# All nine tap products kept in SBUF, planes 6 and 7 added by GpSimd ahead of the fold's reader, other places in the schedule

## The chip, the cores and the metric

The kernel runs on one core of a Trainium2 chip. The metric is the device time in microseconds of one execution, the median of several runs. The core has TensorE (matmuls, results in PSUM), VectorE, ScalarE, GpSimd, and SyncE (SP), which only issues DMAs here. Sixteen DMA engines serve all queues. Each engine works through its own instruction queue in order; semaphores tie the queues together.

## What is computed

The input x has the shape 32 x 64 x 56 x 56 in float32. Two layers are applied, each to a group-normalised copy of its input and added to it:

```python
def _L0_conv_ref(x, ...):                 # binary depthwise + pointwise
    h = sign(x)
    h = depthwise_conv3x3(h, sign(dw_weight))
    h = sign(bn1(prelu(h, prelu1_a)))
    h = einsum('bchw,oc->bohw', h, sign(pw_weight))
    h = bn2(prelu(h, prelu2_a))
    return h + x

def _L1_conv_ref(x, W, b):                # involution: 9 filters per pixel and channel
    filters = einsum('bchw,oc->bohw', x, W) + b       # 64 -> 64*9 channels
    patches = _extract_patches(x)                     # the 9 shifted copies of x
    return sum(patches * filters, over the 9 taps)

x = x + _L0_conv_ref(_gn(x), ...)
x = x + _L1_conv_ref(_gn(x), W, b)
```

The change concerns the last line alone: the sum over the nine taps, and the mean that is added back so that `x` and the result of `_L1_conv_ref(_gn(x))` come out of one sum.

## The kernel before, in words

Two images of 64 channels fill the 128 partitions; that is a *tile*, and there are 16 (`TILES`). A tile has 3136 pixels per partition and is worked in four *quarters* of 784 pixels (`QUARTERS`, `QP`). A quarter has nine taps (`KK`), so a tile has 36 *units*, and unit g of the whole program is one tap of one quarter. Quarters are numbered through, 0 to 63 (`g` in the functions below).

For each unit, TensorE makes 784 filter values per partition in one of four PSUM slots (`unit`, L478), and VectorE makes the product (filter + bias) x shifted q in one instruction (`product`, L946). q is the normalised input of the second layer, and `mirror` is a copy of it with the two images' partitions exchanged, made by four DMAs a tile on SP. Products go to `prod[:, g % BUFS, k, :]`, nine planes of 784 float32 in each of three buffers (`BUFS`).

The nine planes have to be added. That is shared out:

- `fold` (L368): GpSimd issues a DMA that adds planes 0 to 2 onto planes 3 to 5 inside SBUF (1176 KB). It waits for product 5 of the quarter.
- Three quarters of a tile (`POOLED = 1, 2, 3`, in all tiles but the last; `on_pool`): product 8 goes to plane 8, ScalarE adds the mean to it (`add_mean`), GpSimd adds planes 6 to 8 onto 3 to 5 in one instruction of 2352 elements (`add_wide`, L386), then plane 5 onto 3 (`add35`, L399), then 3 + 4 into `ob` (`final`, L410).
- The other quarter (`is_kept`): product 8 is left in its PSUM slot. VectorE adds it and the mean to plane 7 (`pair`, L960), GpSimd adds plane 7 onto 6 (`add_early`, L377), planes 5 and 6 onto 3 and 4 (`add_wide`, L392, 1568 elements), and 3 + 4 into `ob`.
- The last tile goes other ways: in quarters 60 and 61 TensorE adds planes 6 and 7 in PSUM (`SUMMED_LAST`), quarter 62 is kept, and quarter 63 is finished by TensorE and VectorE (`add_to_last`, `last_quarter`).

`add_wide` waits for `folded`, the landing of the quarter's fold. VectorE's product 3 of quarter g waits for `summed` of quarter g - 3, that is for `final`, since it overwrites a buffer; its product 0 waits for that quarter's fold.

What sets the order: every engine's program is a loop over units, and each step of each tile is written into the loop at a unit given by a table. For the steps of a quarter that is a delay behind its first unit (`FOLD_DELAY`, `EARLY_ADD_DELAY`, `MEAN_DELAY`, `WIDE_ADD_DELAY`, `LATE_ADD_DELAY`, `OUT_DELAY`), for the steps that lead up to q (sum, mean, signs, the four depthwise and pointwise jobs, the second statistics) a place relative to the tile's first unit (`COURSE`, and `EARLY` for tiles 0 to 2). These places set the order in each queue and no time.

SP's queue: `store` sends two quarters of `ob` (784 KB) once the second is summed; `mirror_half` sends two of the mirror DMAs; `load` fetches the input of a tile three ahead (1568 KB). The load stands right behind the store of quarters 0 and 1, so that it is issued when quarter 1 of a tile is summed.

The first layer runs on the same engines for the tile ahead: TensorE's depthwise (L521) and pointwise matmuls (L540, L553), ScalarE's activations (all through L581), VectorE's residual add (L917).

Of the kernel before, what the change touches and what calls it, by code (L numbers as in the profile page):

```python
# [19 lines left out]
def preact_involution_kernel(nc, x, dw, a1, gam1, bet1, mu1, var1, pw, a2, gam2, bet2, mu2, var2, W, b, out):  # L20
    B, C, H, WD = x.shape
    KK = 9
# [21 lines left out]
    with ExitStack() as ctx:  # L44
# [153 lines left out]
        def on_pool(g):  # L198
            return g % QUARTERS in POOLED and g < (TILES - 1) * QUARTERS

        def in_banks(g):

            return g % QUARTERS in (SUMMED if g < (TILES - 1) * QUARTERS else SUMMED_LAST)
# [146 lines left out]
        def _(pool):  # L350
# [13 lines left out]
            def fold(t, qq):  # L364
# [4 lines left out]
                               max_dma_last_dim=6 * QP).then_inc(folded[g % BUFS], 16)  # L369

            def add_early(t, qq):
                g = quarter(t, qq)
                pr = planes(g)

                if is_kept(g):
                    pool.wait_ge(paired, kept(g))
                    pool.tensor_tensor(pr[6], pr[6], pr[7], ALU.add).then_inc(summed67, 1)  # L377

            def add_wide(t, qq):
                g = quarter(t, qq)  # L380
                pr = prod[:, g % BUFS, :, :]

                pool.wait_ge(folded[g % BUFS], 16 * (g // BUFS + 1))
                if on_pool(g):
                    pool.wait_ge(mean_added, with_mean(g))
                    pool.tensor_tensor(pr[:, 3:6, :], pr[:, 3:6, :], pr[:, 6:9, :], ALU.add).then_inc(summed_wide, 1)  # L386
                else:
                    if in_banks(g):
                        pool.wait_ge(mean_added, with_mean(g))
                    else:  # L390
                        pool.wait_ge(summed67, kept(g))
                    pool.tensor_tensor(pr[:, 3:5, :], pr[:, 3:5, :], pr[:, 5:7, :], ALU.add).then_inc(summed_wide, 1)  # L392

            def add35(t, qq):
                g = quarter(t, qq)
                pr = planes(g)
                if on_pool(g):
                    pool.wait_ge(summed_wide, g + 1)
                    pool.tensor_tensor(pr[3], pr[3], pr[5], ALU.add).then_inc(summed35, 1)  # L399

            def final(t, qq):
# [6 lines left out]
                else:  # L408
                    pool.wait_ge(summed_wide, g + 1)
                pool.tensor_tensor(ob[:, qq, :], pr[3], pr[4], ALU.add).then_inc(summed, 1)  # L410

            for g in units:
                for what, delay in ((fold, FOLD_DELAY), (add_early, EARLY_ADD_DELAY), (add_wide, WIDE_ADD_DELAY),
                                    (add35, LATE_ADD_DELAY), (final, OUT_DELAY)):
# [588 lines left out]
COURSE = {  # L1003
    'load': -106,
    'sum0': -73,
    'mean0': -70,
    'sign0': -68,
    'square0': -64,
    'var0': -62,
    'root0': -62,  # L1010
    'invert0': -61,
    'scales0': -59,
    'inv_z': -57,
    'ratio': -55,
    'job0': -56,
    'job1': -43,
    'job2': -32,
    'job3': -27,
    'sum1': -20,
    'mean1': -19,  # L1020
    'square1': -13,
    'var1': -11,
    'root1': -10,
    'invert1': -10,
    'q0': -8,
    'q1': -4,
    'b4': -1,
}
EARLY = {
    0: {  # L1030
        'sum0': -71,
        'mean0': -105,
        'sign0': -68,
        'square0': -68,
        'var0': -66,
        'root0': -62,
        'invert0': -64,
        'scales0': -62,
        'inv_z': -60,
        'ratio': -60,  # L1040
        'job0': -65,
        'job1': -64,
        'job2': -59,
        'job3': -58,
        'sum1': -52,
        'mean1': -48,
        'square1': -47,
        'var1': -45,
        'root1': -45,
        'invert1': -45,  # L1050
        'q0': -44,
        'q1': -43,
        'b4': -40},
    1: {
        'sum0': -99,
        'mean0': -98,
        'sign0': -86,
        'square0': -82,
        'var0': -82,
        'root0': -82,  # L1060
        'invert0': -80,
        'scales0': -75,
        'inv_z': -36,
        'ratio': -36,
        'job0': -39,
        'job1': -29,
# [3 lines left out]
        'mean1': -10,  # L1070
        'square1': -8,
        'var1': -9,
        'root1': -8,
        'invert1': -8,
        'q0': -8,
        'q1': -8,
        'b4': 0},
    2: {
        'sum0': -62,
        'mean0': -59,  # L1080
        'sign0': -58,
        'square0': -53,
        'var0': -49,
        'root0': -48,
        'invert0': -47,
        'scales0': -47,
        'inv_z': -44,
        'ratio': -43,
        'job0': -42,
        'job1': -37,  # L1090
# [4 lines left out]
PROLOGUE = {  # L1095
    'bias': -52,
    'turn_w': -41,
    'copy_w': -45,
    'signs_rest': -43,
    'square_0': -58,  # L1100
    'square_1': -54,
    'square_2': -52,
    'square_3': -50,
}

AB_DELAY = 2
RELU_DELAY = 6
ADD_TO_LAST = {30: (0,), 31: (1,), 32: (2,), 35: (3, 4, 5)}

PW_DELAY = 6  # L1110
# [12 lines left out]
TAKE_DELAY = 15  # L1123
DW_OVER = 4

OUT_DELAY = 27

# [22 lines left out]
```

## Time and profile before

| | us |
|---|---|
| median of 3 runs (720.22 to 720.34) | 720.24 |
| the profiled execution | 720.51 |
| its span | 718.6 |
| TensorE busy | 623.5 |
| VectorE busy | 657.9 |
| ScalarE busy | 553.6 |
| GpSimd busy | 603.3 |

The span is the time from the first to the last instruction of the profiled execution. Busy time is what the engine's records cover; a short piece of one record can lie over the next, because an instruction may be taken up before its predecessor has ended. So the step from start to start is often shorter than the duration: 0.94 us for VectorE's products of 1.03 us (three in a row take 2.91). On GpSimd, the records after a DMA issue start about 0.4 us before the engine is free for them and are longer by as much.

### The profile page before, as it was taken

The page shows a single profiled execution, that of the slowest core. Times are in us where ns is not written, and L with a number is a line of the kernel's source. Part 1 is how long each engine was busy: PE and PEld are TensorE (multiplying, and loading weights), DVE is VectorE, ACT ScalarE, POOL GpSimd, SP SyncE. Part 2 cuts the span into 40 slices and gives each one's busy share as a digit, 9 for nine tenths or more (in the row PEclk, how much of TensorE's full clock was granted, in tenths as well). Part 3 has the DMA queues.
Part 4 walks back from the last instruction along what each step waited for, and adds up shares of the span by engine and source line. Part 5 has one row for each costly group of instructions (what it writes and reads, how often), then busy time and mean ns, then how long its engine had stood idle before and what let it go on. Part 6 is the DMA issues. An engine that isn't in the chain of part 4 may idle for free.

```text
span 718.6 us, 18827 instructions
## 1 busy us (share of the span) xinstructions
PE 623.5 (87%) x8017; PEld 254.4 (35%) x8017; DVE 657.9 (92%) x998; ACT 553.6 (77%) x822; POOL 603.3 (84%) x264
## 2 busy tenths in 40 slices
PE   2539889899998989899898989899999989899897
PEld 1224333333333334343333334333333334342333
DVE  3729879999999999999999999999999999999886
ACT  6885998897979788887978898897979888836110
POOL 2002658899999999989899999999999999999896
PEclk9859989999999999999999999999999999999899
DMA  5225767899999999998999999999999997998884
GB/s 202 87 58 148 131 153 196 190 251 207 227 226 196 233 203 245 205 252 187 230 219 182 244 204 250 206 246 215 223 229 193 240 202 162 203 191 176 193 172 136
DMA packets 34280, 142.11 MB, mean 198 GB/s; under 512 B 3348, under 2 KB 11540, under 8 KB 32276
## 3 DMA queue, kind: packets, MB, share of 16 engines
q0 software_dynamic: 17232, 75.87, 58.3%
q1 hardware_dynamic: 16940, 65.03, 27.8%
q8 instruction: 63, 1.03, 0.5%
q14 instruction: 21, 0.17, 0.1%
q10 hardware_dynamic: 24, 0.00, 0.0%
HBM read 26.03 MB, written 25.69 MB: 72 GB/s over the span
## 4 chain that ended last, share of the span: by engine, by line
POOL 48%; DVE 30%; ACT 7%; issue 6%; PE 4%; DMA 3%; SPq 1%; POOLq 0%; DVEq 0%; ACTq 0%
DVE prod L946 25%; POOL prod L386 17%; POOL ob L410 10%; POOL prod L399 10%; POOL prod L368 6%; POOL prod L377 3%; DVE xb L917 3%; PE tap_ps L478 3%; DMA mirror<-q 2%; ACT unused L581 2%; POOL prod L392 2%; ACT st L581 1%; ACT signs L581 1%; ACT ab L581 1%; DMA xb<-in_x_dram 1%
## 5 line engine op out<-in xcount | busy, mean ns | idle before, releaser
L478 PE MATMUL tap_ps<-q,w_t 64*64 64x392 f32 x2304 | 472.1, 506 | 52.1 <-DMA mirror<-q 20.5
L946 DVE SCALAR_TENSOR_TENSOR prod<-tap_ps,bias,q 128x784 f32<-128x784 f32 x493 | 487.4, 1026 | 31.4 <-PE tap_ps L478 26.0
L478 PE MATMUL tap_ps<-mirror,w_t 64*64 64x392 f32 x2304 | 467.4, 507 | 0.0
L478 PEld LDWEIGHTS tap_ps<-q,w_t 64*64 64x64 f32 x2304 | 151.2, 134 | 263.1 <-DVE prod L946 172.6
L386 POOL TENSOR_TENSOR prod<-prod 128x2352 f32<-128x2352 f32 x45 | 240.2, 5337 | 0.0
L368 POOL DMA_DIRECT2D prod<-prod x63 | 75.0, 1190 | 91.3 <-DVE prod L946 91.0
L521 PE MATMUL tap_ps<-signs,dw_diag 64*64 64x392 bf16 x2304 | 135.5, 342 | 9.8 <-DVE dw_diag L846 1.8
L478 PEld LDWEIGHTS tap_ps<-mirror,w_t 64*64 64x64 f32 x2304 | 139.4, 134 | 0.4 <-issue 0.4
L581 ACT ACTIVATE ab<-tap_ps,col 128x784 bf16<-128x784 f32 x128 | 120.5, 993 | 18.1 <-PE tap_ps L521 18.0
L410 POOL TENSOR_TENSOR ob<-prod 128x784 f32<-128x784 f32 x63 | 124.8, 1981 | 6.8 <-POOL prod L399 0.5
L581 ACT ACTIVATE st<-st 128x1 f32<-128x1 f32 x368 | 88.6, 252 | 36.5 <-DVE st L794 24.7
L521 PEld LDWEIGHTS tap_ps<-signs,dw_diag 64*64 64x64 bf16 x2304 | 67.8, 110 | 106.7 <-issue 61.9
L399 POOL TENSOR_TENSOR prod<-prod 128x784 f32<-128x784 f32 x45 | 103.8, 2306 | 0.0
L581 ACT ACTIVATE unused<-xb,st 128x3136 bf16<-128x3136 f32 x31 | 91.6, 2953 | 0.5
L581 ACT ACTIVATE tap_ps<-tap_ps,col 128x784 f32<-128x784 f32 x64 | 61.7, 967 | 18.1 <-PE tap_ps L540 18.1
L917 DVE SCALAR_TENSOR_TENSOR xb<-tap_ps,st,xb 128x784 f32<-128x784 f32 x64 | 65.4, 1024 | 1.8 <-PE tap_ps L553 1.7
L946 DVE SCALAR_TENSOR_TENSOR prod<-tap_ps,st,q 128x784 f32<-128x784 f32 x64 | 65.6, 1025 | 0.1
L392 POOL TENSOR_TENSOR prod<-prod 128x1568 f32<-128x1568 f32 x18 | 65.0, 3609 | 0.0
L581 ACT ACTIVATE q<-xb,st 128x1568 f32<-128x1568 f32 x32 | 54.1, 1697 | 0.5
L581 ACT ACTIVATE signs<-xb,st 128x3136 bf16<-128x3136 f32 (+5 forms) x20 | 47.4, 2387 | 0.5
L581 ACT ACTIVATE prod<-prod,st 128x784 f32<-128x784 f32 x45 | 42.3, 940 | 2.8 <-DVE prod L946 2.8
L581 ACT ACTIVATE unused<-xb 128x3136 bf16<-128x3136 f32 (+1 forms) x16 | 42.4, 2648 | 1.5 <-DMA xb<-in_x_dram 1.5
(117 smaller groups left out, 309.5 us busy)
## 6 DMA issues: line engine op xcount, KB each, us to landing
prod<-prod POOLq DMA_DIRECT2D x63, 1176.0 KB, 10.1
out_dram<-ob SPq DMA_DIRECT2D x31, 784.0 KB, 7.4
xb<-in_x_dram SPq DMA_DIRECT2D x15, 1568.0 KB, 15.7
mirror<-q SPq DMA_DIRECT2D x64, 203.0 KB, 4.3
xb<-in_x_dram SPq DMA_DIRECT2D x2, 784.0 KB, 5.8
out_dram<-ob SPq DMA_DIRECT2D x2, 392.0 KB, 2.3
prod<-in_L_conv_W_dram SPq DMA_DIRECT2D x1, 288.0 KB
prod<-in_L_conv_pw_weight_dram SPq DMA_DIRECT2D x1, 32.0 KB
```

Source lines behind the costliest of these rows:

```text
L368: pool.dma_start(prod[:, g % BUFS, 3:6, :], prod[:, g % BUFS, 0:3, :], accum_op=ALU.add, max_dma_last_dim=6 * QP).then_inc(folded[g % BUFS ...
L377: pool.tensor_tensor(pr[6], pr[6], pr[7], ALU.add).then_inc(summed67, 1)
L386: pool.tensor_tensor(pr[:, 3:6, :], pr[:, 3:6, :], pr[:, 6:9, :], ALU.add).then_inc(summed_wide, 1)
L392: pool.tensor_tensor(pr[:, 3:5, :], pr[:, 3:5, :], pr[:, 5:7, :], ALU.add).then_inc(summed_wide, 1)
L399: pool.tensor_tensor(pr[3], pr[3], pr[5], ALU.add).then_inc(summed35, 1)
L410: pool.tensor_tensor(ob[:, qq, :], pr[3], pr[4], ALU.add).then_inc(summed, 1)
L478: mm = pe.matmul(rows3(tap_ps[to, slot, side, 0:CH]), w_t[own, k, :], moving, start=True, stop=True)
L521: mm = pe.matmul(rows3(banks[to, image, 0:CH]), dw_diag[own, k, own], signs[own, t.par, first:first + ROWS, dx:dx + WD], start=(k == 0), s ...
L581: return nc.scalar.activation(o, i, f, **kw)
L917: v.scalar_tensor_tensor(xj, tap_ps[:, slot, :, 0:CH], s_(t, RATIO), xj, ALU.mult, ALU.add, accum_out=sums[:, t.par, j:j + 1]).then_inc(x1 ...
L946: v.scalar_tensor_tensor(place.rearrange("p j (a b) -> p j a b", b=WD), psum.rearrange("p j (a b) -> p j a b", b=WD), s_(t, B4) if k == 4 ...
```

## The change

All four quarters of tiles 0 to 14 are now treated alike (`POOLED = PAIRED = 0, 1, 2, 3`). Product 8 always goes to plane 8 and ScalarE adds the mean to it. `pair` on VectorE remains for the last tile only. GpSimd adds plane 7 onto 6 as soon as product 7 is there (784 elements), then, after the fold, planes 5 and 6 onto 3 and 4 (1568), then plane 8 onto 3 (784), then 3 + 4 into `ob` (784). `in_fours` and `fold_four` are new too, but `FOURS` is empty, so they do nothing. The delays and most places change; the last tile's ways do not.

```diff
             def add_early(t, qq):
                 g = quarter(t, qq)
                 pr = planes(g)
 
+                if in_pairs(g):
+                    pool.wait_ge(prod_done, KK * g + 8)
+                    pool.tensor_tensor(pr[6], pr[6], pr[7], ALU.add).then_inc(summed67, 1)
                 if is_kept(g):
                     pool.wait_ge(paired, kept(g))
                     pool.tensor_tensor(pr[6], pr[6], pr[7], ALU.add).then_inc(summed67, 1)
...
                 pool.wait_ge(folded[g % BUFS], 16 * (g // BUFS + 1))
-                if on_pool(g):
+                elif on_pool(g) and not in_pairs(g):
                     pool.wait_ge(mean_added, with_mean(g))
                     pool.tensor_tensor(pr[:, 3:6, :], pr[:, 3:6, :], pr[:, 6:9, :], ALU.add).then_inc(summed_wide, 1)
...
-                        pool.wait_ge(summed67, kept(g))
+                        pool.wait_ge(summed67, paired_early(g))
                     pool.tensor_tensor(pr[:, 3:5, :], pr[:, 3:5, :], pr[:, 5:7, :], ALU.add).then_inc(summed_wide, 1)
...
-                if on_pool(g):
+                elif in_pairs(g):
+                    pool.wait_ge(summed_wide, g + 1)
+                    pool.wait_ge(mean_added, with_mean(g))
+                    pool.tensor_tensor(pr[3], pr[3], pr[8], ALU.add).then_inc(summed35, 1)
+                elif on_pool(g):
                     pool.wait_ge(summed_wide, g + 1)
                     pool.tensor_tensor(pr[3], pr[3], pr[5], ALU.add).then_inc(summed35, 1)
...
-FOLD_DELAY = 4
-EARLY_ADD_DELAY = 12
-MEAN_DELAY = 13
-WIDE_ADD_DELAY = 19
-LATE_ADD_DELAY = 25
-POOLED = 1, 2, 3
+FOLD_DELAY = 6
+EARLY_ADD_DELAY = 10
+MEAN_DELAY = 11
+WIDE_ADD_DELAY = 17
+LATE_ADD_DELAY = 19
+POOLED = 0, 1, 2, 3
+FOURS = ()
+PAIRED = 0, 1, 2, 3
...
-OUT_DELAY = 27
+OUT_DELAY = 24
```

In `COURSE` most places move by one to four units: `load` from -106 to -95, `sum1` from -20 to -19, `mean1` from -19 to -16, `square1` from -13 to -15, `root1` from -10 to -13, `q0` from -8 to -9, `b4` from -1 to -8.

On GpSimd, a steady tile before. The DMA row is `fold` of quarter q, the 784 rows onto `prod` are `add35` (L399) or `add_early` (L377), those of 1568 and 2352 elements `add_wide`, those onto `ob` `final`:

```order
L368 DMA prod<-prod 128x2x1176
L399 TENSOR_TENSOR prod<-prod 128x784
L410 TENSOR_TENSOR ob<-prod 128x784
L392 TENSOR_TENSOR prod<-prod 128x1568
L368 DMA prod<-prod 128x2x1176
L410 TENSOR_TENSOR ob<-prod 128x784
L386 TENSOR_TENSOR prod<-prod 128x2352
L368 DMA prod<-prod 128x2x1176
L399 TENSOR_TENSOR prod<-prod 128x784
L410 TENSOR_TENSOR ob<-prod 128x784
L386 TENSOR_TENSOR prod<-prod 128x2352
```

The same engine and place now (L380 is `fold`, L442 `final`, L416 `add_wide`, L396 `add_early`, L428 `add35`), two of the quarters' rounds:

```order
L380 DMA prod<-prod 128x2x1176
L442 TENSOR_TENSOR ob<-prod 128x784
L416 TENSOR_TENSOR prod<-prod 128x1568
L396 TENSOR_TENSOR prod<-prod 128x784
L428 TENSOR_TENSOR prod<-prod 128x784
L380 DMA prod<-prod 128x2x1176
L442 TENSOR_TENSOR ob<-prod 128x784
L416 TENSOR_TENSOR prod<-prod 128x1568
L396 TENSOR_TENSOR prod<-prod 128x784
L428 TENSOR_TENSOR prod<-prod 128x784
```

Each round is: fold of quarter q, `final` of q - 2, `add_wide` of q - 1, `add_early` of q, `add35` of q - 1. Before, `add_wide` of q - 1 also stood between fold q and fold q + 1, but the rounds differed in length, and `add35` and `final` of q - 2 stood directly one behind the other.

On SP the steady round now reads (L344 is `load`, L331 `store`, L339 `mirror_half`):

```order
L344 DMA xb<-in_x_dram 128x3136
L331 DMA out_dram<-ob 128x1568
L339 DMA mirror<-q 64x2x406 x4
L331 DMA out_dram<-ob 128x1568
L344 DMA xb<-in_x_dram 128x3136
```

This is the order that it had before; the load still stands right behind the store of quarters 0 and 1.

## Rows read from the trace of the kernel before

**Rows 1.** The page, part 1: busy us, share of the span, instructions.
```profile
PE 623.5 (87%) x8017; PEld 254.4 (35%) x8017; DVE 657.9 (92%) x998; ACT 553.6 (77%) x822; POOL 603.3 (84%) x264
```

**Rows 2.** Groups by line and form: names, shapes, count, busy us, mean ns, idle before.
```profile
L946 DVE SCALAR_TENSOR_TENSOR prod<-tap_ps,bias,q 128x784 f32<-128x784 f32 x493 | 487.4, 1026 | 31.4 <-PE tap_ps L478 26.0 <-POOL ob L410 4.7
...
L581 ACT ACTIVATE prod<-prod,st 128x784 f32<-128x784 f32 x45 | 42.3, 940 | 2.8 <-DVE prod L946 2.8
...
L960 DVE SCALAR_TENSOR_TENSOR prod<-tap_ps,st,prod 128x784 f32<-128x784 f32 x17 | 17.4, 1025 | 0.0
```

**Rows 3.** GpSimd's timeline, one tile: start us, duration, line, names, idle before.
```profile
585.79 1.20 POOL L368 DMA_DIRECT2D prod<-prod  x1 [1.17 <-DVE prod L946]
586.57 2.32 POOL L399 TENSOR_TENSOR prod<-prod 128x784 f32<-128x784 f32 x1
589.03 1.87 POOL L410 TENSOR_TENSOR ob<-prod 128x784 f32<-128x784 f32 x1
...
596.01 1.17 POOL L368 DMA_DIRECT2D prod<-prod  x1
...
606.18 1.85 POOL L377 TENSOR_TENSOR prod<-prod 128x784 f32<-128x784 f32 x1
607.98 1.16 POOL L368 DMA_DIRECT2D prod<-prod  x1
...
613.03 3.54 POOL L392 TENSOR_TENSOR prod<-prod 128x1568 f32<-128x1568 f32 x1
616.51 1.16 POOL L368 DMA_DIRECT2D prod<-prod  x1
...
625.89 1.20 POOL L368 DMA_DIRECT2D prod<-prod  x1 [1.18 <-DVE prod L946]
```

**Rows 4.** VectorE's waits (us in total, times, longest), and one in its timeline.
```profile
DVE prod L946 <- POOL ob L410: 4.7, 8, 1.4
...
588.88 1.03 DVE L946 SCALAR_TENSOR_TENSOR prod<-tap_ps,bias,q 128x784 f32<-128x784 f32 x1 [0.56 <-PE tap_ps L478]
```

**Rows 5.** Windows: busy us of each engine, granted clock, DMA share, GB/s.
```profile
467.00:488.00 21.00, 19.87 (x284) 8.55 (x288) 20.89 (x31) 18.90 (x27) 20.71 (x9) 1.00 1.01 241
```

**Rows 6.** The folds (L368): all; then issue and landing of folds 39 and 40.
```profile
DMA to landing us min/median/max: 8.7/10.1/16.1
...
465.48 1.20 POOL L368 DMA_DIRECT2D prod<-prod  x1 [1.17 <-DVE prod L946]
DMA to landing us min/median/max: 10.8/10.8/10.8
475.69 1.20 POOL L368 DMA_DIRECT2D prod<-prod  x1
DMA to landing us min/median/max: 15.4/15.4/15.4
```

**Rows 7.** SP's timeline beside fold 39; DMA queues from 476 to 480 us.
```profile
470.99 1.80 SPq L332 DMA_DIRECT2D xb<-in_x_dram  x1
...
q1 hardware_dynamic: 205, 1.38, 103.7%
```

**Rows 8.** GpSimd's timeline near the end, from fold 62 on.
```profile
696.93 1.19 POOL L368 DMA_DIRECT2D prod<-prod  x1
697.70 2.30 POOL L410 TENSOR_TENSOR ob<-prod 128x784 f32<-128x784 f32 x1
699.51 3.96 POOL L392 TENSOR_TENSOR prod<-prod 128x1568 f32<-128x1568 f32 x1
702.99 2.28 POOL L377 TENSOR_TENSOR prod<-prod 128x784 f32<-128x784 f32 x1
```

**Rows 9.** GpSimd's timeline: folds 8, 60 and 61.
```profile
151.01 1.16 POOL L368 DMA_DIRECT2D prod<-prod  x1
...
678.27 1.20 POOL L368 DMA_DIRECT2D prod<-prod  x1 [2.64 <-DVE prod L946]
...
688.44 1.20 POOL L368 DMA_DIRECT2D prod<-prod  x1
```

More of the change, by code:

```diff
@@ L199, in on_pool, with in_fours, in_pairs, paired_early @@
             return g % QUARTERS in POOLED and g < (TILES - 1) * QUARTERS
+        def in_fours(g):
+            return on_pool(g) and g % QUARTERS in FOURS
+        def in_pairs(g):
+            return on_pool(g) and g % QUARTERS in PAIRED
+        def paired_early(g):
+            return sum(is_kept(n) or in_pairs(n) for n in range(g + 1))
         def in_banks(g):
@@ L369, in fold, with fold_four @@
                                max_dma_last_dim=6 * QP).then_inc(folded[g % BUFS], 16)
+            def fold_four(t, qq):
+                g = quarter(t, qq)
+                wait(pool, prod_done, KK * g + 8)
+                pool.dma_start(prod[:, g % BUFS, 4:8, :], prod[:, g % BUFS, 0:4, :], accum_op=ALU.add,
+                               max_dma_last_dim=8 * QP).then_inc(folded[g % BUFS], 16)
             def add_early(t, qq):
@@ L409, in final @@
                     pool.wait_ge(summed_wide, g + 1)
-                pool.tensor_tensor(ob[:, qq, :], pr[3], pr[4], ALU.add).then_inc(summed, 1)
+                pool.tensor_tensor(ob[:, qq, :], pr[5] if in_fours(g) else pr[3], pr[4], ALU.add).then_inc(summed, 1)
             for g in units:
-                for what, delay in ((fold, FOLD_DELAY), (add_early, EARLY_ADD_DELAY), (add_wide, WIDE_ADD_DELAY),
+                for t, qq in quarters(g, FOLD_DELAY):
+                    if not in_fours(quarter(t, qq)) and not (t.last and qq == QUARTERS - 1):
+                        fold(t, qq)
+                for t, qq in quarters(g, FOLD_FOUR_DELAY):
+                    if in_fours(quarter(t, qq)):
+                        fold_four(t, qq)
+                for what, delay in ((add_early, EARLY_ADD_DELAY), (add_wide, WIDE_ADD_DELAY),
                                     (add35, LATE_ADD_DELAY), (final, OUT_DELAY)):
@@ L1070 @@
         'mean1': -10,
[L1071 to L1073 removed]
+        'square1': -9,
+        'var1': -8,
+        'root1': -9,
         'invert1': -8,
         'q0': -8,
[L1076 to L1089 removed]
+        'q1': -5,
+        'b4': -1},
+    2: {
+        'sum0': -63,
+        'mean0': -60,
+        'sign0': -56,
+        'square0': -55,
+        'var0': -50,
+        'root0': -51,
+        'invert0': -48,
+        'scales0': -46,
+        'inv_z': -41,
+        'ratio': -34,
+        'job0': -40,
         'job1': -37,
```

109 lines of the change are left out of this document (58 added, 51 removed).

## The prediction

> **What bounds the kernel now.** I read the busy shares first [rows 1]: VectorE 92%, TensorE 87%, GpSimd 84%, so none of them is plainly the bound, and the question is who waits for whom. The costliest groups [rows 2] give the price of each step. The GpSimd timeline over one of the last steady tiles [rows 3] is the most telling view. From the fold issued at 585.79 to the one at 625.89, 40.10 us, GpSimd sits idle only once, 1.18 us, waiting for a VectorE product. Within a tile, the three quarters that use the 2352-element add need about 10.2 us of GpSimd each (585.79 to 596.01), more than VectorE needs for nine products, so VectorE is held up. The quarter with the 1568-element add needs only 8.53 us (607.98 to 616.51), so GpSimd catches up and ends by waiting for VectorE. The loop is thus closed half by GpSimd, half by VectorE. VectorE's own waits for GpSimd's last add are only 4.7 us in the whole run [rows 4]: the two are balanced.
>
> A third resource shows only in the windows. In a tile in which the input of a later tile is loaded, the 16 DMA engines are full: share 1.01 over 467 to 488 us [rows 5]. The folds (1176 KB) land after 8.7 us at best, 10.1 in the median, 16.1 at worst [rows 6]. I number them by quarter, 0 to 62. The long ones are always the first fold of a tile: all 11 of folds 8, 12, ..., 48 took 13.7 to 16.1 us. Fold 40, issued at 475.69, took 15.4; fold 39 before it, issued at 465.48, took 10.8 [rows 6]. The reason is in SP's timeline [rows 7]: when the quarter-1 sum is written during the cycle of fold 39, SP issues a 784 KB store and at once the 1568 KB load. In the slice 476 to 480 the hardware queue then has 103.7% of the engines and the fold's queue nothing [rows 7]. Nobody waits for this today, because the fold's reader comes late: fold 40's reader runs after fold 41, 11.95 us later, plus 5.4 us of other adds (the same places as 596.01 and 613.03 in [rows 3]: 17.0 us after the issue).
>
> **The change part by part.**
> *VectorE.* In tiles 0 to 14 the pair add disappears: 15 at 1025 ns [rows 2], 0.94 us start to start, so 0.94 us per tile. ScalarE gets 15 more mean additions of 940 ns [rows 2], some 14 us on an engine that is busy 77% [rows 1]. It lies beside other work as long as ScalarE's statistics keep their place; I cost it at nothing. TensorE does the same work and gets one PSUM slot back sooner.
>
> *GpSimd.* Each quarter of tiles 0 to 14 is now 784 + 1568 + 784 + 784 elements plus one fold issue. The end of the kernel shows exactly this sequence, without a wait [rows 8]. Fold issued at 696.93, the 784 add after it ends at 697.70 + 2.30 = 700.00: 3.07. The 1568 add ends at 699.51 + 3.96 = 703.47: 3.47. The next 784 add ends at 702.99 + 2.28 = 705.27: 1.80. A further one would be 1.80 too. Sum 10.14, less 0.07 by which the next instruction starts before the last has ended (606.18 + 1.85 = 608.03, next at 607.98 [rows 3]; elsewhere up to 0.07): **10.07 us a quarter, 40.3 a tile**. The order of the adds puts another instruction between each one and the one that it depends on, so the 0.14 us gap that stands between 586.57 + 2.32 = 588.89 and 589.03 goes. If a fold issue could not overlap at all it would be 10.2, which I keep as the upper bound. Now a tile is 38.9 us of GpSimd work plus 1.18 of wait. VectorE would need 40.1, less 0.56 of waiting for TensorE and 0.59 for GpSimd (4.7 us in 8 waits [rows 4]), less 0.94: 38.0. So GpSimd becomes the bound of every steady tile, VectorE leads it by up to about 4 us, and small stalls of VectorE (the mirror DMAs) no longer cost anything.
>
> Base of the sum, with no other waits: from fold 8 at 151.01 to fold 60 at 678.27 are 527.26 us now [rows 9], 40.56 a tile with the stalls. At 52 × 10.07 = 523.6 that is **−3.6** (at 10.2: +3.1). Before fold 8 VectorE is the bound, with two pair adds of 0.94 fewer; GpSimd's chain of 10.07 takes over from fold 5 on, which leaves **−0.8** (bounds −1.9 and +2, since the retuned places of the first tiles move the statistics either way). In the last tile GpSimd needs 3.07 + 3.47 + 1.80 − 0.07 = 8.3 from fold 60 to 61 and 6.5 to fold 62, now 10.17 and 8.49 [rows 9, 8]; VectorE, having led, permits most of this: **−3.5** (bounds 0 and −3.9). From fold 62 on all is as before.
>
> *The fold's reader.* This is the term that decides. In the new order the 1568 add of quarter q always runs after fold q+1 and one 784 add: 10.07 + 3.07 = 13.1 us after its own fold was issued, with no exception. A fold of 10.1 us, and the 10.8 of fold 39, fit. The first fold of a loading tile does not. Its landing is better counted from the fold ahead of it: 10.21 + 15.4 = 25.6 us for folds 39 and 40 (25.0 to 26.5 for the eleven, median 25.3), while the reader comes at 2 × 10.07 + 3.07 = 23.2. Can the landing come sooner? The load is issued after the final add, which now follows the fold issue directly: 3.4 us after it instead of 5.5 (465.48 to 470.99 [rows 6, 7]). But the engines are full from the moment fold 39 moves until fold 40 has landed [rows 5]. An earlier load only slows fold 39 in exchange; the sum of the bytes (two folds, a store, a load) stays, and so does its end. So GpSimd waits 25.3 − 23.2 = **2.1 us in each of 11 tiles: +23** (from 1.8 to 3.3 each by the eleven; none, if the earlier load fills an idle DMA engine after all). It is not hidden: GpSimd is the bound and its queue is in order, so the early add, the 784 add, the next fold and the final add that frees the buffer for VectorE's product 3 all stand behind the waiting instruction.
>
> The Trainium skill, DMA: Bandwidth & Descriptors, section "Anatomy of one DMA — SWDGE (gpsimd) path", gives about 2.0 us plus bytes over 436e3; for a fold that is an estimate of 4.8 us, and by it no reader would ever wait. The trace disagrees: 8.7 us is the shortest here [rows 6].
>
> **The sum.** Profiled span 718.6 − 0.8 − 3.6 − 3.5 + 23 = 733.7. The profiled run took 720.51, 1.9 above its span, and the median 720.24 is 1.64 above it; so **735.3, rounded to 735**.
>
> **The rivals.**
> *No new wait, faster.* If the landing of the first fold follows the load, which now starts 2 us sooner, it comes at 23.3 instead of 25.3 and the reader at 23.2 finds it done. Then 718.6 − 7.9 + 1.64 = **712.3**. For it: the 16 engines are not evenly loaded at the end of such a stretch, and the landing is set by the slowest. Against it: the share of 1.01. It decides at 0.7 us of wait per loading tile: 11 × 0.7 is what the rest gains, and from there on the kernel is slower. A small wait of 0.5 to 0.9 gives 718 to 722, the same as before.
> *GpSimd alone is too slow.* At 10.2 us a quarter and no wait for folds: 718.6 − 0.8 + 3.1 − 2 = 718.9, **720.5**, no change; with both, 742.
> *The wait is longer.* If the earlier load holds fold 39 itself beyond 13.1 us, or a store or the mirror DMAs, issued sooner because VectorE leads, delay a second fold in the tile, it is 3 to 4 us a tile: **745 to 756**.
> *The VectorE gain in full.* If the loop followed VectorE, 15 × 0.94 = 14 us would go: 706. It needs GpSimd under 9.6 us a quarter, and no row shows such a sum; I leave it at 2%.
>
> **How the numbers follow.** The waiting fold at 1 us or more per loading tile: 0.57 (722 to 746). Longer waits: 0.08. GpSimd slower without fold waits or with small ones: 0.10 (717 to 724). No wait at all: 0.25 (706 to 716). A difference under 0.2% (1.4 us) can't be told from no change in a measurement of this kernel. So faster 0.28, same 0.07, slower 0.65. The range is 712 to 746: below it lie 8 in 100, above it 8. The forecast's own range is 722 to 746.
>
> **What the changed profile would show.** Right: VectorE busy near 642 us, the pair add left only in the last tile; fold issues of GpSimd 10.07 us apart in the last two tiles without a load, and one interval of about 12 in each loading tile, with idle time before the 1568 add for which the only late releaser is the fold's DMA; VectorE waiting for the final add or TensorE for VectorE every quarter. Wrong: no idle time before the 1568 add and 40.3 us a tile means the DMA argument fails and the time is near 712; equal intervals of 10.2 or more mean that the step of GpSimd was mis-sized; idle GpSimd before folds means VectorE or ScalarE is late, and neither sum holds.

## The result, and the profile after

| | before | after |
|---|---|---|
| median, us | 720.29 (4 runs, 720.22 to 720.35) | 729.32 (4 runs, 727.42 to 731.18) |
| the profiled execution | 720.51 | 727.42 |
| its span | 718.6 | 725.6 |
| from fold 8 to fold 60 | 527.26 | 534.88 |

The ratio is 1.012, with a 95% interval of 1.0103 to 1.0137: slower by 9.0 us. The forecast of 735 had the sign and was 5.7 us too high. Its main reason, a wait for the fold, is not what the trace shows.

Page, busy shares and chain that ended last (share of the span by engine), kernel after; the lines of before are [rows 1]:

```profile
PE 622.0 (86%) x8017; PEld 274.8 (38%) x8017; DVE 644.5 (89%) x983; ACT 568.4 (78%) x837; POOL 635.6 (88%) x324
...
DVE 43%; PE 23%; DMA 13%; issue 10%; ACT 10%; SPq 1%; DVEq 0%; ACTq 0%
```

VectorE lost 13.4 us of work and GpSimd took on 32.3, both as the change says. But GpSimd is not on the chain that ended last. VectorE, TensorE and the DMA are. Which DMA, the groups and the waits say (us in total, times, longest), kernel after:

```profile
L984 DVE SCALAR_TENSOR_TENSOR prod<-tap_ps,bias,q 128x784 f32<-128x784 f32 x508 | 500.5, 1024 | 49.9 <-PE tap_ps L516 47.6
L516 PE MATMUL tap_ps<-q,w_t 64*64 64x392 f32 x2304 | 481.7, 515 | 58.4 <-DMA mirror<-q 47.7
```

```profile
DVE prod L984 <- PE tap_ps L516: 49.9, 26, 8.6
PE tap_ps L516 <- DMA mirror<-q: 47.7, 16, 12.0
```

TensorE's wait for the mirror DMA, by which a tile's matmuls with the second input start, comes once a tile. VectorE waits behind it. Beside [rows 2], where VectorE waited 26.0 us for TensorE, this is 24 us more. The fold's reader, which carried the forecast, waits 2.6 us in the whole run. The same views cut to the steady stretch, fold 8 to fold 60, kernel after (waits, then the window: PE, PEld, DVE, ACT and POOL busy, TensorE's granted clock as a share of 2.4 GHz, DMA share, GB/s):

```profile
PE tap_ps L516 <- DMA mirror<-q: 34.5, 13, 4.1
...
DVE prod L984 <- PE tap_ps L516: 32.8, 15, 3.4
...
POOL prod L416 <- DMA prod<-prod: 2.6, 6, 0.7
POOL prod L380 <- DVE prod L984: 2.5, 5, 0.6
```

```profile
150.15:685.03 534.88, 481.77 (x6328) 213.41 (x6324) 500.24 (x717) 440.37 (x648) 529.43 (x262) 0.96 0.94 212
```

The same stretch of before has 11.8 us of VectorE waiting for TensorE's products (14 times, longest 2.3). There are 13 tiles in it, so after has about one such stall a tile (15), of 2.2 us on average. GpSimd works 529.43 of 534.88 us: it is still nearly the bound, idle for 5.45 us, half of it for folds and half for VectorE's products.

Here is one tile in which an input is loaded. GpSimd's timeline, kernel after (start us, duration, line, names, idle before):

```profile
357.53 1.20 POOL L380 DMA_DIRECT2D prod<-prod  x1 [0.47 <-DVE prod L984]
358.31 2.32 POOL L442 TENSOR_TENSOR ob<-prod 128x784 f32<-128x784 f32 x1
360.12 4.00 POOL L416 TENSOR_TENSOR prod<-prod 128x1568 f32<-128x1568 f32 x1
363.62 2.31 POOL L396 TENSOR_TENSOR prod<-prod 128x784 f32<-128x784 f32 x1
365.43 2.31 POOL L428 TENSOR_TENSOR prod<-prod 128x784 f32<-128x784 f32 x1
367.24 1.66 POOL L380 DMA_DIRECT2D prod<-prod  x1
...
377.89 1.25 POOL L380 DMA_DIRECT2D prod<-prod  x1
...
387.65 1.64 POOL L380 DMA_DIRECT2D prod<-prod  x1
...
395.56 2.72 POOL L428 TENSOR_TENSOR prod<-prod 128x784 f32<-128x784 f32 x1
398.88 1.20 POOL L380 DMA_DIRECT2D prod<-prod  x1 [0.61 <-DVE prod L984]
```

A round is best read by its ends: the last add of a round ends at 365.43 + 2.31 = 367.74, and 395.56 + 2.72 = 398.28 is three rounds later: 10.18 a round. The parts of one, from the ends of these rows: 1.16 for issuing the fold, then 1.8 to 1.9, 3.48, 1.81 and 1.82 for the adds, **10.15 us** together.

The third fold of the tile goes out at 377.89. SP issues the mirror DMAs of the next tile at 383.19, beside it. SP's timeline, then the chain that ended last, then the DMA queues in the slices 384 to 385 and 386 to 387 (packets, MB, share of the 16 engines), kernel after:

```profile
383.19 5.75 SPq L339 DMA_DIRECT2D mirror<-q  x4
```

```profile
383.83 6.11 DMA mirror<-q
...
390.07 1.62 PE tap_ps L516 x8
...
391.81 1.03 DVE prod L984
```

```profile
q0 software_dynamic: 37, 0.17, 101.3%
...
q1 hardware_dynamic: 78, 0.13, 59.3%
q0 software_dynamic: 17, 0.01, 7.8%
```

From 384 to 385 only q0, the folds' queue, moves bytes. The mirror's queue, q1, has no row there; it appears from 386 on, when the fold is through. So the mirror lands after 6.1 us, where its transfer alone, in the first tile with no fold about, took 3.1:

```profile
47.86 3.13 DMA mirror<-q
```

VectorE then starts its next product 2.76 us late:

```profile
391.81 1.03 DVE L984 SCALAR_TENSOR_TENSOR prod<-tap_ps,bias,q 128x784 f32<-128x784 f32 x1 [2.76 <-PE tap_ps L516]
```

A part of these 2.76 us is TensorE's clock. Windows of 1 us, kernel after (the number behind the five engines is the granted clock, 0.50 is 1.2 GHz):

```profile
389.00:390.00 1.00, 0.00 (x0) 0.00 (x0) 0.05 (x1) 1.00 (x1) 1.00 (x2) 0.68 0.92 210
390.00:391.00 1.00, 0.93 (x8) 0.55 (x12) 0.00 (x0) 1.00 (x1) 1.00 (x2) 0.50 1.06 225
```

TensorE had been idle for 2.61 us when the mirror was there at last, and its clock had fallen in that time. The eight matmuls of the next filter took 1.62 us, and VectorE started 1.74 us after the first of them. In the kernel before, at the same mirror, TensorE was idle for 1.66 us, the clock stayed at 1.00, and VectorE started 1.05 us after the first matmul:

```profile
387.39 0.51 PE L478 MATMUL tap_ps<-q,w_t 64*64 64x392 f32 x1 [1.66 <-DVE prod L946]
388.44 1.03 DVE L946 SCALAR_TENSOR_TENSOR prod<-tap_ps,bias,q 128x784 f32<-128x784 f32 x1 [1.15 <-PE tap_ps L478]
387.00:388.00 1.00, 0.61 (x8) 0.39 (x12) 0.28 (x1) 1.00 (x2) 1.00 (x1) 1.00 1.05 193
```

So the lower clock makes this stall 0.7 us longer. In windows of 1 us from fold 8 to fold 60, the clock is at 0.50 behind the stall in 12 of the 13 tiles of after, and in 2 of before. An estimate of its share is 12 × 0.7 = 8 of the 32.8 us of stalls.

In the kernel before, the same mirror was issued between two folds. SP's timeline and the DMA queues from 384 to 386 us, kernel before; the folds next to it were issued at 375.4 and 385.1:

```profile
382.36 6.37 SPq L327 DMA_DIRECT2D mirror<-q  x4
```

```profile
q1 hardware_dynamic: 243, 0.35, 65.0%
q0 software_dynamic: 2, 0.00, 1.2%
```

There the mirror left 7.0 us after the third fold of the tile, whose bytes were nearly through; in after it left 5.3 us behind that fold. The short round of 8.53 us [rows 3] had brought the third fold forward (experiments 4 and 11, which bring that round back, bring the place back too). With four equal rounds of 10.15 us it stands over the mirror in every tile: from tile 3 on, the mirror leaves 3.4 to 6.2 us behind a fold, in before 6.0 to 7.0.

### The profile page after: what moved, and what is told of

The parts are those of the page before. It is cut to its first block, busy times and chain, and to the rows that moved or that the text cites. A ratio compares the mean times of both kernels' runs of the same rounds, so it can differ in the third digit from the quotient of the medians.

```text
span 725.6 us, 18947 instructions
## 1 busy us (share of the span) xinstructions
PE 622.0 (86%) x8017; PEld 274.8 (38%) x8017; DVE 644.5 (89%) x983; ACT 568.4 (78%) x837; POOL 635.6 (88%) x324
## 3 DMA queue, kind: packets, MB, share of 16 engines
q0 software_dynamic: 17232, 75.87, 57.0%
## 4 chain that ended last, share of the span: by engine, by line
DVE 43%; PE 23%; DMA 13%; issue 10%; ACT 10%; SPq 1%; DVEq 0%; ACTq 0%
DVE prod L984 33%; PE tap_ps L516 15%; DMA mirror<-q 12%; DVE xb L955 7%; ACT ab L619 4%; PE tap_ps L559 4%; ACT unused L619 3%; ACT st L619 2%; PE tap_ps L538 1%; PE tap_ps L578 1%; DVE st L832 1%; DMA xb<-in_x_dram 1%; PE tap_ps L525 1%; ACT signs L619 1%; PE tap_ps L591 1%
## 5 line engine op out<-in xcount | busy, mean ns | idle before, releaser
L984 DVE SCALAR_TENSOR_TENSOR prod<-tap_ps,bias,q 128x784 f32<-128x784 f32 x508 | 500.5, 1024 | 49.9 <-PE tap_ps L516 47.6
L516 PE MATMUL tap_ps<-q,w_t 64*64 64x392 f32 x2304 | 481.7, 515 | 58.4 <-DMA mirror<-q 47.7
L516 PE MATMUL tap_ps<-mirror,w_t 64*64 64x392 f32 x2304 | 474.7, 515 | 0.0
L416 POOL TENSOR_TENSOR prod<-prod 128x1568 f32<-128x1568 f32 x63 | 257.9, 4094 | 2.6 <-DMA prod<-prod 2.6
L516 PEld LDWEIGHTS tap_ps<-q,w_t 64*64 64x64 f32 x2304 | 163.5, 137 | 248.1 <-DVE prod L984 160.6
L442 POOL TENSOR_TENSOR ob<-prod 128x784 f32<-128x784 f32 x63 | 162.7, 2583 | 0.1
L380 POOL DMA_DIRECT2D prod<-prod x63 | 98.1, 1558 | 72.0 <-DVE prod L984 71.6
L396 POOL TENSOR_TENSOR prod<-prod 128x784 f32<-128x784 f32 x60 | 144.8, 2413 | 1.3 <-DVE prod L984 1.3
L428 POOL TENSOR_TENSOR prod<-prod 128x784 f32<-128x784 f32 x60 | 144.3, 2406 | 0.1
L559 PEld LDWEIGHTS tap_ps<-signs,dw_diag 64*64 64x64 bf16 x2304 | 74.3, 108 | 95.0 <-issue 68.5
L619 ACT ACTIVATE prod<-prod,st 128x784 f32<-128x784 f32 x60 | 56.3, 939 | 4.3 <-DVE prod L984 4.3
## 6 DMA issues: line engine op xcount, KB each, us to landing
prod<-prod POOLq DMA_DIRECT2D x63, 1176.0 KB, 11.2
```

Source lines behind the costliest of these rows:

```text
L380: pool.dma_start(prod[:, g % BUFS, 3:6, :], prod[:, g % BUFS, 0:3, :], accum_op=ALU.add, max_dma_last_dim=6 * QP).then_inc(folded[g % BUFS ...
L428: pool.tensor_tensor(pr[3], pr[3], pr[8], ALU.add).then_inc(summed35, 1)
L442: pool.tensor_tensor(ob[:, qq, :], pr[5] if in_fours(g) else pr[3], pr[4], ALU.add).then_inc(summed, 1)
L516: mm = pe.matmul(rows3(tap_ps[to, slot, side, 0:CH]), w_t[own, k, :], moving, start=True, stop=True)
L559: mm = pe.matmul(rows3(banks[to, image, 0:CH]), dw_diag[own, k, own], signs[own, t.par, first:first + ROWS, dx:dx + WD], start=(k == 0), s ...
L619: return nc.scalar.activation(o, i, f, **kw)
```

## The experiments

Each is an edit of the kernel after, unless said otherwise. Ratios are to the kernel before on the same chip, whose medians there were 719.9 to 720.7 us.

**1. The load made small.** What is the fold's reader worth, and what does the load cost at all?

```diff
-                sp.dma_start(xb[:, t.x_slot, :], x_t[t.n]).then_inc(x_loaded[t.x_slot], 16)
+                sp.dma_start(xb[:, t.x_slot, 0:NPIX // 8], x_t[t.n, :, 0:NPIX // 8]).then_inc(x_loaded[t.x_slot], 16)
```

> The changed kernel, but from tile 3 on each load of an input tile fetches an eighth of it (the rest of the buffer keeps older values). Theory B (the load starves the fold, whose reader on GpSimd waits): the wait of the 1568 add for the fold, 2.6 us in all in the changed kernel, goes, and no more than that: 1 to 3 us faster; had the prediction's 2.1 us a tile been there it would be 20. Theory A: the load comes after the mirror DMAs, so the wait for the mirror stays at 40 us or more and the time at 725 to 729.

Measured: 725.55 us, ratio 1.0068 (1.0046 to 1.0091). GpSimd no longer waits for any fold, and 4 to 5 us are gone against after (729.3 and 730.4 in two measurements). TensorE still waits 44.6 us for the mirror. So the load's bytes cost 4 to 5 us, where the forecast had put 23 on them, and about half of the loss (4.9 us against before) stands without them. Not all of the 4 to 5 us is the fold's reader: VectorE's waits for TensorE in the stretch fell too, from 32.8 to 28.9 us.

**2. The mirror made small** (one of seven rows, from tile 2 on).

```diff
+                    rows = ROWS if t.n < 2 else 1
-                    sp.dma_start(mirror[own, t.par, 2 * half:2 * half + 2, :, :],
-                                 of_quarters[:, 2 * half:2 * half + 2, side, :, :]).then_inc(mirrored[half], 16)
+                    sp.dma_start(mirror[own, t.par, 2 * half:2 * half + 2, 0:rows, :],
+                                 of_quarters[:, 2 * half:2 * half + 2, side, 0:rows, :]).then_inc(mirrored[half], 16)
```

> The changed kernel, but from tile 2 on each mirror DMA copies one row in seven (the filter values made from the mirror are then those of older rows; all instructions and waits stay). Theory A (the mirror DMAs sit behind a fold and TensorE waits for them, 47.7 us in the changed kernel's trace against 20.5 before): that wait shrinks to under 20 us and the time falls from about 728 to GpSimd's own pace, 4 x 10.15 us = 40.6 a tile instead of 41.1: 719 to 722 us. Theory B (GpSimd's fold reader waits, the term of the prediction): nothing changes, 726 us or more. Theory C (GpSimd alone sets the pace and the wait of TensorE is its shadow): within 2 us of the changed kernel.

Measured: 721.12 us, ratio 1.001 (0.9996 to 1.0023). Nearly all of the loss is gone. The window from fold 8 to fold 60, and the wait, kernel with the small mirror:

```profile
151.19:679.19 528.00, 479.25 (x6325) 211.51 (x6325) 500.56 (x717) 439.64 (x648) 527.98 (x262) 0.97 0.89 196
...
PE tap_ps L517 <- DMA mirror<-q: 39.8, 14, 11.9
```

GpSimd works 527.98 of 528.00 us: 10.15 a round, and it never waits. This is the pure bound of GpSimd's round, and it is 0.7 us longer than the 527.26 us of before [rows 9]. So even where GpSimd never waits the change gains nothing. The second line was not expected: DMAs of one seventh still keep TensorE waiting 39.8 us. In the tile above, the small mirror took 5.34 us; for its first 1.5 us, up to 383, only the fold's queue moved bytes. VectorE's waits for TensorE in the stretch fell only from 32.8 to 25.1 us. That is enough: 38.5 us of work and 1.9 of stall a tile keep VectorE ahead of GpSimd's 40.6.

```profile
381.50 5.34 DMA mirror<-q
```

**3. The old places.** `COURSE`, `EARLY`, `PROLOGUE` and three delays as before, the quarters' ways as after.

```diff
-    'load': -95,
+    'load': -106,
...
-AB_DELAY = 1
+AB_DELAY = 2
-RELU_DELAY = 5
+RELU_DELAY = 6
-PW_DELAY = 5
+PW_DELAY = 6
```

> The changed kernel with the tables COURSE, EARLY and PROLOGUE and the three delays of the first layer (2, 6, 6) as before; the quarters' new way and their new delays stay. If the retuned places help the new way, this is slower than the changed kernel by 2 us or more; if the loss of the change lies in the places (theory D), it is near 720; if it lies in the four equal rounds of GpSimd (theories A and C), within 3 us of 729.

Measured: 738.98 us (4 runs, 733.6 to 743.9), ratio 1.025 (1.019 to 1.0311). Here GpSimd waits 12.3 us for folds, and new waits between TensorE and ScalarE come in (32.4 us in front of the pointwise matmuls of L591, where before had 13.5 at the same place). The new places are thus worth about 9 us to the new ways of the quarters. They are no part of the loss.

**4. Three pooled quarters in the new places.** The ways of the quarters undone, the rest as after.

```diff
-POOLED = 0, 1, 2, 3
+POOLED = 1, 2, 3
-PAIRED = 0, 1, 2, 3
+PAIRED = ()
```

> The changed kernel with one quarter in four kept in PSUM and paired on VectorE again and the 2352-element add in the other three; places and delays as changed. Theories A and C (the quarters' new way costs the time): near the kernel before, 717 to 722. Theory D (the places): near 729. Its order sets another instruction between add35 and final, which saves GpSimd 0.14 us in three rounds, so up to 5 us faster than before is possible where GpSimd holds up VectorE.

Measured: 719.52 us, ratio 0.9983 (0.9971 to 0.9995), against after 0.985 to 0.987. So the new ways cost 10 to 11 us in the same places, and the places alone are worth 0 to 2. GpSimd waits for VectorE's products 23 times here, and TensorE 28.3 us for the mirror. The mirrors leave 6.1 to 6.3 us behind a fold (5.4 in the last tile), and VectorE's waits for TensorE in the stretch are 13.3 us, as against 32.8:

```profile
POOL prod L380 <- DVE prod L984: 95.3, 23, 49.2
...
PE tap_ps L516 <- DMA mirror<-q: 28.3, 12, 11.6
```

**5. The early add shortened** to 16 elements: GpSimd's round is some 1.8 us shorter, the mirror as in after.

```diff
-                    pool.tensor_tensor(pr[6], pr[6], pr[7], ALU.add).then_inc(summed67, 1)
+                    pool.tensor_tensor(pr[6][:, 0:16], pr[6][:, 0:16], pr[7][:, 0:16], ALU.add).then_inc(summed67, 1)
```

> The changed kernel, but GpSimd's early add of plane 7 onto 6 covers 16 elements instead of 784 in the four quarters of tiles 0 to 14 (the rest of plane 7 is left out of the sum). That takes about 1.6 us from each of GpSimd's rounds of 10.15, so GpSimd no longer sets any pace. Theory A (the mirror DMAs behind a fold cost 0.5 us a tile beyond GpSimd's 40.6): the mirror chain stays and the time falls at most a little, 722 to 727, if the folds keep their place beside the mirror DMAs. Theory C (GpSimd alone is the bound): the time falls toward VectorE's 38 us a tile, below 705.

Measured: 715.5 us, ratio 0.9929 (0.9904 to 0.9955). GpSimd's busy time falls by 96.5 us, the time by 14 to 15. That is neither 722 to 727 nor below 705: GpSimd's round and the mirror each held a part. What is left is VectorE's loop with the mirror in it:

```profile
PE 615.2 (86%) x8017; PEld 270.6 (38%) x8017; DVE 644.3 (91%) x983; ACT 567.9 (80%) x837; POOL 539.1 (76%) x324
...
PE tap_ps L516 <- DMA mirror<-q: 31.9, 13, 11.5
```

**6. Both: early add short and mirror small.**

> Both cuts: GpSimd's early add of 16 elements and mirror DMAs of one row in seven from tile 2 on. If GpSimd and the mirror chain are the two bounds and nothing else is near, the pace becomes VectorE's, 38.0 to 39.5 us a tile: 690 to 708. If it stays above 712, something else (ScalarE's statistics, TensorE, the DMA engines) is next at once.

Measured: 694.25 us, ratio 0.9641 (0.9623 to 0.9659). With GpSimd alone relieved 715.5, with the mirror alone relieved 721.1, with both 694.3: two limits that lie within 6 us of each other, and either one hides what the other costs. VectorE is the bound now. The chain that ended last has no more than 4% of DMA:

```profile
DVE 45%; ACT 22%; issue 15%; PE 13%; DMA 4%; SPq 1%; DVEq 0%; ACTq 0%
```

**7. The mirror sooner.** All places of the first layer but the load three units earlier, so that the mirror leaves before the third fold (tile 2 keeps its own).

```diff
-    'q0': -9,
-    'q1': -4,
+    'q0': -12,
+    'q1': -7,
```

> The changed kernel with all places of COURSE but the load three units earlier (tile 2 keeps its old ones), so that q and its mirror DMAs come some 2.8 us sooner against the quarters' folds. Theory A: the wait of TensorE for the mirror, 47.7 us, falls below 30 and GpSimd's 40.6 us a tile is left: 719 to 723. If the steps only move in the queues and still wait for the same data, or VectorE waits for the statistics instead, the time stays at 727 to 731.

Measured: 739.77 us, ratio 1.0283 (1.0255 to 1.0311). The remedy failed, though TensorE's wait for the mirror fell from 47.7 to 31.3 us. The earlier statistics make TensorE and ScalarE wait for each other (29.1 us against 7.8 in after), and the mirror now meets a fold from its start:

```profile
PE tap_ps L591 <- ACT tap_ps L619: 29.1, 20, 4.3
```

```profile
349.07 9.97 DMA mirror<-q
```

Most of the loss lies ahead of the steady stretch: fold 8 is issued at 160.65 us instead of 150.15, and from there to fold 60 it takes 536.55 us, where the two traces of after have 534.88 and 537.74. The edit shifts tile 3 and leaves tile 2, and most of those 10.5 us are lost between folds 3 and 6. So this run says little on what a shift alone would do in the steady tiles.

**8. The same shift with three pooled quarters.**

> As three_pooled (one quarter in four kept and paired on VectorE, places and delays as changed), with the same places three units earlier. Its trace shows 28.3 us of TensorE's waits for the mirror and no steady bound but VectorE. Theory A: another 5 us at most can go, 715 to 719, better than both kernels. If the balance is already VectorE's, within 1 us of three_pooled.

Measured: 745.2 us, ratio 1.0352 (1.0327 to 1.0376). The shift is worse here too, so its cost is not one of the new rounds. Here it costs 11.0 us ahead of fold 8 and 12.9 in the stretch. An order that sends the mirror ahead of the fold and leaves the statistics in peace was not found.

**9. The fold made small** (a quarter of each plane, so that its packets are through in a fourth of the time): does the mirror wait for the fold's bytes?

```diff
-                pool.dma_start(prod[:, g % BUFS, 3:6, :], prod[:, g % BUFS, 0:3, :], accum_op=ALU.add,
+                pool.dma_start(prod[:, g % BUFS, 3:6, 0:QP // 4], prod[:, g % BUFS, 0:3, 0:QP // 4], accum_op=ALU.add,
```

> The changed kernel, but every fold DMA adds only a quarter of each plane (294 KB instead of 1176; the other three quarters of planes 0 to 2 are left out of the sum); mirror DMAs and GpSimd's instructions are whole. Theory A (the mirror DMAs wait behind the fold in flight; 6.1 us to landing in a steady tile against 3.1 without a fold beside them): the landing falls to about 3 to 4 us, TensorE's wait for the mirror from 47.7 to under 25 us, and GpSimd's 40.6 us a tile is left: 717 to 722. If the mirror's landing stays at 6 us, its delay comes from elsewhere (SP, the stores, the statistics) and the time stays at 725 or more.

Measured: 724.27 us, ratio 1.0055 (1.0037 to 1.0072). DMA issues (KB each, median us to landing), waits, the chain that ended last, and the window from 200 to 640 us, kernel with the small fold:

```profile
mirror<-q SPq DMA_DIRECT2D x64, 203.0 KB, 3.2
...
DVE prod L984 <- POOL ob L442: 30.3, 50, 1.6
...
PE tap_ps L516 <- DMA mirror<-q: 13.8, 5, 11.1
...
POOL 60%; issue 17%; ACT 11%; DVE 7%; PE 2%; DMA 2%; SPq 0%; POOLq 0%; ACTq 0%; DVEq 0%
```

```profile
200.00:640.00 440.00, 405.83 (x5308) 154.41 (x5300) 415.96 (x601) 378.39 (x556) 440.00 (x216) 1.00 0.50 125
```

The mirror of full size lands after 3.2 us instead of 4.5 in the median, and the waits for it are gone but for 5. The mirrors leave 2.6 to 4.4 us behind a fold, no later than in after, so it is not their place that changed. The small fold has more packets than the whole one (25296 in all for 17232) and a quarter of the bytes. This shows that it is the fold's transfer that holds the mirror up, and not the number of its packets. The clock stays at 1.00 through the stretch. GpSimd is then busy in every microsecond of the window, and VectorE waits for it about once a quarter, 50 times. That is the picture the prediction had drawn for the time without fold waits. The time is above that of experiment 2, because this fold costs GpSimd 1.25 us of issuing instead of 1.16 (its rows are cut into more pieces; that these are the reason isn't shown), which is 52 × 0.09 = 4.7 us; without that it would be 719.6, an estimate, and agrees with the 721.1 of experiment 2.

**10. The new way in quarter 0 alone of the four** (quarters 1 to 3 add 2352 elements at once).

```diff
-PAIRED = 0, 1, 2, 3
+PAIRED = (0,)
```

> The changed kernel with the new way in quarter 0 of each tile alone; quarters 1 to 3 use the 2352-element add again, places and delays as changed. VectorE has no pair add here either. GpSimd has one instruction less in three rounds (0.16 us each), but add35 stands directly behind the wide add that it waits for (0.1 us each): about 40.2 to 40.5 us a tile. Theory: the time follows GpSimd and the mirror chain, 720 to 729; VectorE's saving of 14 us does not show.

Measured: 723.02 us (12 runs, 721.9 to 728.5), ratio 1.0046 (1.0026 to 1.0067). Three fewer instructions a tile on GpSimd give 6 to 7 us of the 9 to 10 back, and the mirror still costs TensorE 45.8 us.

**11. As 10, but quarter 0 kept on VectorE in every second tile.**

```diff
-            return g % QUARTERS in POOLED and g < (TILES - 1) * QUARTERS
+            return (g % QUARTERS in POOLED and (g % QUARTERS > 0 or g // QUARTERS % 2 == 1)
+                    and g < (TILES - 1) * QUARTERS)
```

> As paired0, but the ninth product of quarter 0 is left in PSUM and paired on VectorE in every second tile, so that half of VectorE's pair adds go: GpSimd 38.4 and 40.3 us in turn, 39.3 on average, VectorE 39.0 and 38.0. If the two engines' balance is what counts, 712 to 718 and the best of all correct kernels here; if the mirror DMAs' place beside a fold decides, 718 to 728, since the folds shift from tile to tile.

Measured: 721.04 us, ratio 1.0012 (0.9994 to 1.003): no difference from before can be told. The profiled run, 725.88 us and the slowest of the 12, holds both phases. In every second tile (176 to 587 us) the mirror leaves 6.2 us behind a fold, and VectorE then waits for TensorE 0 to 1.9 us; in the tiles between it leaves 4.3 to 5.5 us behind, and the wait is 1.7 to 4.0. Sharing the work more finely between the two engines brings nothing beyond 719.5, experiment 4, which is the fastest of the kernels that compute all, by 0.05 to 0.3%.

**12. The kernel after again**, in five rounds.

> The changed kernel unchanged, timed once more beside the kernel before, so that the experiments have a base on chips of their own. It is expected at 727 to 731 us, 1.0 to 1.4% above the kernel before; if it is below 725 here, the differences of small_mirror (721.1), small_load (725.6) and small_fold (724.3) to it have to be read smaller.

Measured: 730.4 us in 5 runs, ratio 1.0135 (1.0115 to 1.0155). TensorE waits 49.5 us for the mirror and GpSimd 3.9 for folds, as in the first trace.

## Why the prediction was right and wrong, step by step

**The bound.** Right that VectorE and GpSimd are balanced before, and that GpSimd would be busy almost throughout (529.43 of 534.88 us). Wrong that this makes it the only bound. VectorE needs 38.5 us a tile (500.24 us in 13 tiles), where the forecast had 38.0, and 32.8 us of stalls make it 41.0; the tile took 41.14. "VectorE leads it by up to about 4 us" left out the stall.

**"Small stalls of VectorE (the mirror DMAs) no longer cost anything".** This term was put at nothing, and that failed. With the mirror small, 8 to 9 us are gone (729.3 and 730.4 against 721.1). Not all of that is VectorE's stalls: of the 6.9 us between the two profiled stretches, 2.5 are GpSimd's waits for products, 2.6 its waits for folds, which go with the mirror's bytes too, 0.3 another wait, and 1.5 longer busy time of GpSimd. I had looked at the stalls' price in the old phases, 11.8 us in the stretch, and took both price and place as fixed. They grew to 32.8, because the rounds became equal and the third fold moved over the mirror's issue, and because TensorE, idle for longer, then went on at the lower clock. How the stall follows the place of the mirror behind the fold, from tile 3 on (us):

| kernel | mirror issued behind a fold by | its first DMA lands after | VectorE's waits for TensorE, stretch |
|---|---|---|---|
| before | 6.0 to 7.0 | 3.0 to 4.1 | 11.8 |
| three pooled quarters (4) | 5.4 to 6.3 | 4.0 to 5.5 | 13.3 |
| after | 3.4 to 6.2 | 5.2 to 7.3 | 32.8 |
| small mirror (2) | 2.9 to 5.8 | 3.8 to 6.5 | 25.1 |
| three units earlier (7) | 0.8 to 2.3 | 8.1 to 9.4 | 25.4 |
| small fold (9) | 2.6 to 4.4 | 2.9 to 4.1 | none |

In experiment 7 the mirror leaves earlier for those that read it, so a landing of 8 to 9 us costs no more there. Experiment 9 shows the cause of the late landing, and experiments 4 and 11 show that the stall goes with the phase. That the phase alone makes before faster isn't shown: the attempt to set it back (7) moved the statistics as well.

**GpSimd's round of 10.07.** It is 10.15, in the trace and, undisturbed, in experiment 2. The parts had been right: 3.07, 3.47, 1.80 and 1.80. The error was to take off 0.07 for overlap from a sum made of differences between ends, which holds the overlap already. 52 × 0.08 = 4.2 us, which turned −3.6 into +0.6 (+0.7 in experiment 2).

**The fold's reader, +23.** This is the largest miss. It is 2.6 to 3.9 us of waiting, and at most 4 to 5 us of time by experiment 1. The reader's place was nearly right: 24.1 us after the fold ahead, not 23.2, since the rounds are longer and GpSimd waits for a product in between. The landing was the error: 387.65 + 11.6 gives one fold, and 398.88 + 12.8 = 411.7 the next, which is 24.0 after the issue of the one ahead, not 25.3. Over the same eleven folds the median is 24.2 us (23.7 to 24.9). The landings of all folds, and of this one (L380), kernel after:

```profile
DMA to landing us min/median/max: 8.7/11.2/14.5
DMA to landing us min/median/max: 12.8/12.8/12.8
```

The median fold is slower than in [rows 6] (11.2 for 10.1) and the slowest is faster (14.5 for 16.1). So "an earlier load only slows fold 39 in exchange" held, but "and so does its end" didn't: from the fold ahead to the landing the DMA engines moved 230 to 236 GB/s, in before 215 to 229, and the end came 1.1 us sooner. The rival had named this as its condition (an idle DMA engine that the load fills); its landing was 23.3, so the truth lies about midway. GpSimd's longer rounds and its waits for products brought the reader later, too, and so only 6 readers waited. The forecast took the share of 1.01 over 21 us for a proof that nothing was left to fill.

**Before fold 8, −0.8.** Right: it was issued at 150.15 against 151.01 [rows 9].

**The last tile, −3.5.** It was +0.2: from fold 60 to the end 40.57 us against 40.33. Folds 61 and 62 follow after 8.56 and 10.18 us, where 8.3 and 6.5 had been expected. GpSimd, kernel after:

```profile
685.03 1.20 POOL L380 DMA_DIRECT2D prod<-prod  x1 [0.30 <-POOL prod L428]
...
693.59 1.22 POOL L380 DMA_DIRECT2D prod<-prod  x1
...
703.77 1.21 POOL L380 DMA_DIRECT2D prod<-prod  x1 [3.60 <-DVE prod L984]
```

GpSimd was ready and waited 3.60 us for VectorE, which had no lead to give. VectorE's lead is the same error as above.

**VectorE and ScalarE.** Right: 644.5 us busy for "near 642", and ScalarE's 14.8 us more cost nothing that shows.

**The sum.** Terms of the span as forecast: −0.8 − 3.6 + 23 − 3.5 = +15.1. As measured: −0.86 + 7.62 + 0.24 = +7.0. The steady stretch thus came out 11.2 us above its forecast without fold waits (7.62 for −3.6): 4.2 for the round, 5.4 of idle time (2.6 for folds, 2.5 for VectorE's products, 0.3 other) and 1.6 of busy time above 52 × 10.15. The total landed in the range because several small terms stood where one large one had been forecast. That is luck: "slower" had rested on the fold's +23, and it came true through the balance between the two engines, for which the same sum had forecast −7.9. One of the recorded signs of being wrong did appear, idle GpSimd ahead of folds (2.5 us in 5 waits in the stretch, 3.60 us at the end), and VectorE's wait for the final add in every quarter, forecast as a sign of being right, did not. The rival's "with both, 742" isn't the sum of its terms either: 720.5 + 23 is 743.5, and with the reader later at 10.2 us a round it is 740.6.

## What to carry to other kernels

Sum an engine's round from ends to ends, once, and if the sum is within 1% of today's, expect little from moving work onto that engine, as here. Before making rounds equal, list what each small, urgent DMA meets in flight at its issue, before and after: a change that moves no DMA in any queue can still put one under a large transfer. Look at the granted clock behind each stall of TensorE: it can make the stall longer than the wait itself. Where two limits lie close together, take each away alone and then both, since either alone shows too little.

## What the runs showed of the hardware

In the tile shown, while a fold's packets moved, the mirror's did not: q1 has no bytes in the slices 384 to 385 and 385 to 386, 1 to 3 us after SP had issued. It is the same the other way round: in before, a load in flight kept the fold's queue at nothing for 4 us [rows 7]. So over such times the two queues did not share the engines evenly; one went through, then the other.

A DMA of one seventh of the bytes (29 KB for 203) still had to wait where a fold was in its way: issued 3.2 us behind a fold it landed after 6.4 us, issued 6.2 us behind one (experiment 6) after 2.8. The full mirror took 7.3 at 3.4 us and 4.0 to 5.1 at 6.2 (experiment 4). So the place in the line costs more than the size. The folds' queue has 17232 packets and 75.87 MB in the page of after, 274 a fold, so about 17 on each of the 16 engines:

```profile
q0 software_dynamic: 17232, 75.87, 57.0%
```

The Trainium skill, DMA: Bandwidth & Descriptors, section "Queues, rings and completion order", says that an engine goes round between the queues but drains a whole packet of one queue before it switches, some 9 to 17 descriptors. If the profile's packets are what that page calls descriptors, an engine's share of a fold is one such packet, and the trace agrees: the mirror waits for what is left of the fold, whatever its own size. Experiment 9 doesn't prove it: the small fold has 402 packets (25296 in all), 25 on each engine, and the mirror landed after 2.9 to 4.1 us, so the bytes ahead count. Whether it is the descriptors or the data of the mirror that stand behind the fold isn't settled.

The issue of an accumulating DMA by GpSimd cost the engine 1.16 us in every round, and 1.25 us for a quarter of the bytes in more packets (experiment 9). Over 52 rounds such a difference is worth 4.7 us.

TensorE's clock was granted at the lower of its two levels, 0.50 or 1.2 GHz, after the stalls at the mirror: eight filter matmuls then took 1.62 us, and VectorE had its operand 0.7 us later than at 2.4 GHz.
